# Last layer of a four-layer kernel: ScalarE copies the spread values out of PSUM, GpSimd makes the key-value products, the scans read them from SBUF

## The reference

```python
r = xr @ Wr; k = xk @ Wk; v = xv @ Wv
w_log = -jnp.exp(time_decay + jnp.tanh(xw @ decay_w1) @ decay_w2)
def fwd_step(S, inp):
    rt, kt, vt, wt = inp
    S = jnp.exp(wt)[..., None] * S + kt[..., None] * vt[..., None, :]
    return (S, jnp.einsum('bhk,bhkv->bhv', rt, S))
def bwd_step(S, inp):
    rt, kt, vt, wt = inp
    y = jnp.einsum('bhk,bhkv->bhv', rt, S)
    S = jnp.exp(wt)[..., None] * (S + kt[..., None] * vt[..., None, :])
    return (S, y)
y = y_f + y_b
y = y * jax.nn.sigmoid(dx @ gate_w + gate_b)   # then a norm over each head, times g, times Wo
```

## Time and profile before

| | us |
|---|---|
| median of 3 runs (lowest, highest) | 2316.47 (2316.39, 2316.59) |
| profiled execution, its own time | 2314.24 |
| its span, first to last instruction | 2312.5 |
| first forward scan of the last layer starts | 1997.20 |
| last backward scan starts | 2268.12 |
| mean granted TensorE clock, share of full speed | 0.945 |

### The profile page before, as it was taken

How to read it: one execution, slowest core, us unless ns; L and a number is a source line. 1 busy time by engine, 2 the same in 40 slices (tenths; PEclk the granted TensorE clock), 3 DMA queues, 4 the chain that set the end, 5 groups by cost and what they waited for, 6 DMA issues and landing times. The chain is left out here.

```text
span 2312.5 us, 56820 instructions
## 1 busy us (share of the span) xinstructions
PE 2062.4 (89%) x22888; PEld 1391.5 (60%) x22888; DVE 1623.5 (70%) x4129; ACT 1283.3 (55%) x2560; POOL 947.6 (41%) x1176
## 2 busy tenths in 40 slices
PE   4679998998999999999999796899999986889886
PEld 2448887996888887888887664344433333334233
DVE  7666664775666676667665563899898936698895
ACT  2247775565777777777776242267676763323323
POOL 2037776664678744665443032111111100154462
PEclk8789999999999999999999797699999997999998
DMA  6311113104011100000000063011111101000000
GB/s 180 106 64 38 39 38 97 50 29 149 21 39 19 35 3 20 2 21 3 3 2 2 16 205 106 16 43 49 38 37 38 40 4 38 0 0 9 0 9 19
DMA packets 77925, 94.14 MB, mean 41 GB/s; under 512 B 10145, under 2 KB 56242, under 8 KB 76002
## 3 DMA queue, kind: packets, MB, share of 16 engines
q1 hardware_dynamic: 64178, 77.23, 11.1%
q0 software_dynamic: 13488, 13.28, 2.9%
HBM read 54.55 MB, written 35.53 MB: 39 GB/s over the span
## 5 line engine op out<-in xcount | busy, mean ns | idle before, releaser
L1166 DVE TENSOR_REDUCE a_parts<-a_S 128x1 f32<-128x512 f32 (+1 forms) x576 | 363.0, 684 | 29.0 <-PE a_S L1050 22.7
L1137 ACT ACTIVATE WA<-a_E 128x1024 f32<-128x1024 f32 (+1 forms) x320 | 283.1, 940 | 117.9 <-PE a_E L1078 58.8
L1042 PE MATMUL a_S<-a_KS,a_QS 54*128 54x512 bf16 (+3 forms) x768 | 189.6, 348 | 31.0 <-DVE a_parts L1166 18.4
L463 POOL TENSOR_SCALAR WA<-WA,a1b_rinv 128x1024 f32<-128x1024 f32 (+3 forms) x192 | 142.5, 761 | 181.8 <-DVE a1b_rinv L802 181.6
L463 POOL TENSOR_SCALAR XR<-XR,a1b_rinv 128x768 f32<-128x768 f32 (+3 forms) x192 | 141.7, 752 | 118.9 <-DVE a1b_rinv L802 118.4
L618 PE MATMUL a1b_O<-a1b_PT,WA 128*64 128x128 f32 x3072 | 189.0, 276 | 0.0
L618 PEld LDWEIGHTS a1b_O<-a1b_PT,WA 128*64 128x64 f32 x3072 | 165.8, 137 | 6.5
L583 PE MATMUL a1b_B<-a1b_Kf,a1b_Qf 64*128 64x512 f32 (+2 forms) x768 | 156.2, 481 | 8.5 <-issue 4.6
L1042 PEld LDWEIGHTS a_S<-a_KS,a_QS 54*128 54x128 bf16 x768 | 58.7, 95 | 172.5 <-DVE a_parts L1166 136.0
L1090 PE MATMUL a_O<-WA,V 128*9 128x512 f32 (+3 forms) x1536 | 154.2, 489 | 0.1
L714 ACT ACTIVATE WA<-WA,a1b_nmax 128x1024 f32<-128x1024 f32 (+3 forms) x192 | 150.4, 792 | 1.3 <-DVE a1b_nmax L784 1.3
(11 more groups left out here) (533 smaller groups left out, 5890.9 us busy)
## 6 DMA issues: line engine op xcount, KB each, us to landing
WA<-in_w SPq DMA_DIRECT2D x8, 1024.0 KB, 9.0
a_QS<-qstack SPq DMA_DIRECT2D x32, 216.0 KB
a_KS<-kstack SPq DMA_DIRECT2D x32, 216.0 KB
a1b_tb<-tab SPq DMA_DIRECT2D x12, 512.0 KB
qstack<-f_parts SPq DMA_DIRECT2D x24, 256.0 KB
kstack<-f_parts SPq DMA_DIRECT2D x24, 256.0 KB
f_slots<-f1r_zrows SPq DMA_DIRECT2D x9, 516.0 KB
f1t_xs<-f_slots SPq DMA_DIRECT2D x9, 516.0 KB, 7.3
```

Of the source, the lines that this page charges most:

```text
L463: pool.tensor_scalar(v, v, rinv[:, e, u, part:part + 1], 1.0, ALU.mult, ALU.mult).then_inc(n_sb, 1)
L1042: ins = pe.matmul(pS[(at + half) % SB][:, lo:lo + n], QS[s][ROW[half], pair, i * P:(i + 1) * P], KS[s][ROW[half], pair, block * P:block * ...
L1137: act.activation(PT[q % NP][:, :, 0:w], pE[q % 2][:, :, 0:w], ACT.Exp).then_inc(e_sb, 1)
L1166: dve.tensor_reduce(peak, pS[at % SB][:, :].rearrange("p (c k) -> p c k", c=n), AX.X, ALU.max)\
```

## The change

Per step, the product of spread values and keys leaves VectorE. ScalarE copies the spread values from PSUM into an SBUF tile (`spread`, two of them, the memory of mdx and mxr), and GpSimd multiplies them with k into an SBUF tile `kv` (two of them), from which both scans read. TensorE's `values(n)` waits for the copy of step n - 2 where it waited for the scans of step n - 2. GpSimd makes the product of step n + 1 ahead of the sum of step n (`weigh`). The sum is written into Sr and multiplied there in place, so that Ss is gone. ScalarE's program of a batch is cut into eight parts with one copy behind each.

```diff
-    pV = kv = [ph.ps(f"V{i}", (P, T)) for i in range(2)]
+    pV = [ph.ps(f"V{i}", (P, T)) for i in range(2)]
+    NK, NV = 2, 2
+    kv = tile("kv", True)
+    flat = [m[:, :, :].rearrange("p s t -> p (s t)")[:, 0:T] for m in (mdx, mxr, mxk)]
+    spread = flat[0:2]
...
+            def weigh(n):
+                if n >= NS:
+                    return
+                b, v = divmod(n, HK)
+                if v == 0:
+                    pool.wait_ge(emptied["k"], 2 * b + 2)
+                pool.wait_ge(spread_sb, n + 1)
+                if n >= NK:
+                    pool.wait_ge(scanned, n - NK + 1)
+                elif n == 0:
+                    pool.wait_ge(l_delta, EARLY - 1)
+                pool.tensor_tensor(kv[n % NK][:, :], spread[n % NV][:, :], k[b % 2][:, :], ALU.mult).then_inc(kv_sb, 1)
+
+            weigh(0)
+            weigh(1)
             for b in range(B):
                 for v in range(HK):
                     n, s = b * HK + v, v % 2
+                    if n:
+                        weigh(n + 1)
                     if v == 0:
                         pool.wait_ge(emptied["r"], 2 * b + 2)
                     if n >= 2:
                         pool.wait_ge(y_ps, n - 1)
                     pool.wait_ge(scanned, n + 1)
-                    if n:
-                        pool.wait_ge(sr_sb, n)
-                    pool.tensor_tensor(Ss[:, :], Sf[s][:, :], Sb[:, s, 1:T + 1], ALU.add).then_inc(sum_sb, 1)
+                    pool.tensor_tensor(Sr[s][:, :], Sf[s][:, :], Sb[:, s, 1:T + 1], ALU.add).then_inc(sum_sb, 1)
                     pool.wait_ge(sum_sb, n + 1)
-                    pool.tensor_tensor(Sr[s][:, :], Ss[:, :], r[b % 2][:, :], ALU.mult).then_inc(sr_sb, 1)
+                    pool.tensor_tensor(Sr[s][:, :], Sr[s][:, :], r[b % 2][:, :], ALU.mult).then_inc(sr_sb, 1)
...
                 if n >= 2:
-                    pe.wait_ge(scanned, n - 1)
+                    pe.wait_ge(spread_sb, n - 1)
...
+            def spread_values(n):
+                if n >= NS:
+                    return
+                act.wait_ge(v_ps, n + 1)
+                if n >= NV:
+                    act.wait_ge(kv_sb, n - NV + 1)
+                else:
+                    act.wait_ge((l_mixed, l_rk)[n], EARLY)
+                act.copy(spread[n % NV][:, :], pV[n % 2][:, :]).then_inc(spread_sb, 1)
...
+                for v in range(HK):
+                    n = b * HK + v
+                    if v == 0:
+                        if b + 1 < B:
+                            begin(b + 1)
+                        if b:
+                            evacuate("cen", b - 1)
+                        if b + 1 < B:
+                            for kind in ("t5a", "t5b", "gate"):
+                                evacuate(kind, b + 1)
+                    if v == 1 and b:
+                        evacuate("var", b - 1)
+                        deviation(b - 1)
+                    if v == 2 and b + 1 < B:
+                        evacuate("d1", b + 1)
...
+                    if 4 <= v <= 6 and b + 1 < B:
+                        evacuate("krg"[v - 4], b + 1)
+                    if b + 1 < B or v + 2 < HK:
+                        spread_values(n + 2)
...
-                    dve.wait_ge(v_ps, n + 1)
                     if v == 0:
-                        dve.wait_ge(emptied["k"], 2 * b + 2)
                         dve.wait_ge(dec_sb, b + 1)
-                    dve.tensor_tensor(kv[s][:, :], pV[s][:, :], k[b % 2][:, :], ALU.mult).then_inc(kv_ps, 1)
                     if n >= 2:
                         dve.wait_ge(sum_sb, n - 1)
-                    dve.wait_ge(kv_ps, n + 1)
-                    dve.tensor_tensor_scan(Sf[s][:, :], dec[b % 2][:, :], kv[s][:, :], 0.0, ALU.mult, ALU.add)
-                    dve.tensor_tensor_scan(Sb[:, s, T - 1::-1], kv[s][:, ::-1], dec[b % 2][:, ::-1], 0.0,
+                    dve.wait_ge(kv_sb, n + 1)
+                    dve.tensor_tensor_scan(Sf[s][:, :], dec[b % 2][:, :], kv[n % NK][:, :], 0.0, ALU.mult, ALU.add)
+                    dve.tensor_tensor_scan(Sb[:, s, T - 1::-1], kv[n % NK][:, ::-1], dec[b % 2][:, ::-1], 0.0,
                                            ALU.add, ALU.mult).then_inc(scanned, 1)
```

More of the change, by code:

```diff
@@ L2112, in wkv @@
     Sf, Sr = (tile(n, True) for n in ("Sf", "Sr"))
-    Ss = tile("Ss")
     Sb = ph.sb("Sb", [P, 2, T + 1])
@@ L2124, in wkv @@
     mdx, mxr, mxk = (ph.sb(n, [P, 3, CH]) for n in ("mdx", "mxr", "mxk"))
+    flat = [m[:, :, :].rearrange("p s t -> p (s t)")[:, 0:T] for m in (mdx, mxr, mxk)]
     mkr = [Sf[0][:, 0:CH], Sf[0][:, CH:T], Sf[1][:, 0:CH]]
     mdelta = [Sr[0][:, 0:CH], Sr[0][:, CH:T], Sr[1][:, 0:CH]]
-    msig = [Sf[1][:, CH:T], Sr[1][:, CH:T], Ss[:, 0:CH]]
+    msig = [Sf[1][:, CH:T], Sr[1][:, CH:T], kv[0][:, 0:CH]]
+    spread = flat[0:2]
     low = [t[:, 0:CH] for t in (*pV, pY)]
@@ L2131, in wkv @@
         ph.sem(n) for n in ("ldx", "lmixed", "lrk", "lrelu", "lk2", "lsig", "lv", "ldelta", "ltr", "lx"))
-    stored = ph.sem("stored")
+    stored, spread_sb = ph.sem("stored"), ph.sem("spreadsb")
     rows_out = out.rearrange("(n p) d -> p n d", p=P)
@@ L2136, in wkv @@
     dx1, dx2, xv1, ln_sb, de_sb, yc_sb = (ph.sem(n) for n in ("dx1", "dx2", "xv1", "lnsb", "desb", "ycsb"))
-    v_ps, kv_ps, scanned, sum_sb, sr_sb, y_ps, c_ps = (
-        ph.sem(n) for n in ("vps", "kvps", "scanned", "sumsb", "srsb", "yps", "cps"))
+    v_ps, kv_sb, scanned, sum_sb, sr_sb, y_ps, c_ps = (
+        ph.sem(n) for n in ("vps", "kvsb", "scanned", "sumsb", "srsb", "yps", "cps"))
     KINDS = ("t5a", "t5b", "gate", "m_w", "m_k", "d1", "m_v", "d2", "m_r", "k", "m_g", "r", "g", "cen", "var", "out")
@@ L2434, in _ @@
             evacuate("g", 0)
+            spread_values(0)
+            spread_values(1)
             for b in range(B):
[L2436 to L2454, removed]
+                for v in range(HK):
[13 more added lines that the diff above has]
+                        evacuate("d1", b + 1)
+                    if v == 3:
+                        if b:
+                            shape(b - 1)
+                        if b + 1 < B:
+                            evacuate("d2", b + 1)
+                            decay(b + 1)
+                    if 4 <= v <= 6 and b + 1 < B:
+                        evacuate("krg"[v - 4], b + 1)
+                    if b + 1 < B or v + 2 < HK:
+                        spread_values(n + 2)
             evacuate("cen", B - 1)
@@ L2587, in _ @@
             gated(B - 1)
+            dve.wait_ge(kv_sb, NS)
             interpolate(4)
```

## The result

| | before | changed |
|---|---|---|
| median, us | 2316.43 (4 runs) | 2413.05 (4 runs, 2412.36 to 2413.82) |
| ratio, 95% interval | | 1.0425, [1.0411, 1.0438] |
| profiled execution's span, us | 2312.5 | 2411.3 |

The account below looks back on a forecast made before the run. VectorE was taken to bound the loop, except for a chain through all engines at batch starts. 25.7 + 2 x 23.1 + 38.5 = 110.4 us on 2314.24, plus 2.2 for the median, gave 2427 us; range 2385 to 2465.

Parts of the forecast that it names:

- The step that decides: Scans in the last layer's loop, now with two SBUF inputs, and SBUF-reading GpSimd instructions exclude each other by whole instructions.
- The cost of one step: Scan loop: five instructions of VectorE and GpSimd take turns at one port, 10.8 us a step (10.4 to 11.4).
- Steps 2 to 7 of batch 1: Six steps of 10.8 us plus normalisation and xv additions on the port: 68.0 us against 49.4, +18.6.
- The first two steps of a batch: Batch start, from scan v = 0 to scan v = 2: 31.6 us against 27.1, +4.5 (bounds +3 to +9).
- The walk: Batch start followed instruction by instruction from the end of product kv of v = 0; scan v = 2 starts at 31 to 33.
- Batch 3: Last batch, no next one to prepare: 50.0 us become 8 x 10.8 + 2.1 = 88.5, +38.5, the largest term.
- the first scan: Start of the loop: later by ScalarE's copy and GpSimd's product less VectorE's product, 2.3 us.
- batch 0: First batch of the loop: 92.7 us against 69.3, with steps 2 to 7 +20.4 and its start +3.
- the likeliest case: Scans and GpSimd exclude each other by whole instructions in the loop: 2427 us, bounds 2413 to 2455, chance 0.76.
- TensorE as a bound: Rival: TensorE at the lower clock presses on the steps, 5 to 25 us more a batch, 2455 us named, chance 0.08.
- The first rival: Scans don't take the port: about -6 us in each of three batches, 2306 us, faster by 0.5%, chance 0.11.
- Signs to look for: Expected profile: scans over 4 us, GpSimd maxima of 4, 10.5 to 11 between forward scans, VectorE busier, TensorE awaiting GpSimd.

Follow-up runs that it names:

- The run nearest to it: Changed kernel with both scans reading the spread values in PSUM instead of GpSimd's product in SBUF, TensorE waiting for the scans, product unused: 2326.86 us, ratio 1.0053.

## Why the prediction was right, and where it was not

- **The step that decides** held. The choice to carry the exclusion, seen only for additions and similar operations, over to scans was right: two runs that move the scans' operand between PSUM and SBUF, and no instruction from one engine to another, show it from both sides (+39 us into SBUF, -86 us out of it).
- **The cost of one step** was 10.8 us and measured 10.52 where five instructions follow strictly. The terms came to 10.66, and 0.14 was added for an order that didn't come. The scans took 2.15 and 2.16 us where 2.09 and 2.07 were counted, the multiplications 2.13 where 2.21 were, the sum 1.95 for 2.00, and the 0.08 between two instructions of one engine was not paid.
- **Steps 2 to 7 of batch 1**: 64.8 for 68.0. Six steps of 10.52 and the 3.2 us of other two-input work would be 66.3. But only the last two of the six have that length: from forward scan to forward scan they took 10.9, 15.4, 7.8, 9.6, 10.5 and 10.5 us. The rest is attributed, untested, to stretches in which VectorE works out of PSUM while GpSimd runs ahead.
- **The first two steps of a batch**: 34.2 for 31.6, inside the bounds of +3 to +9. The walk held up to the scans of v = 1: `begin` ended 18.8 us after the product (18.6 forecast), both scans 23.2 after it (23.1). The predicted stall of GpSimd was there too: it waited 14.4 us for the copy behind the evacuation of `gate`, and that copy waited last for TensorE's values. But the mix of w ended at 34.4, not near 31.5: VectorE waited 9.6 us for m_w's matmul, which began 12.6 us after the last matmuls of `t5a` began; before it was 9.9. Of these 2.8 us the walk lacked two things. TensorE waited 1.4 us for ScalarE's evacuation of `var`, which now stands behind the new copy; and matmuls ran longer at the lower level (3.62 us for 2.70 in one group; the granted clock of the two steps was 0.73, and 0.94 before). Before:

```profile
2079.72 1.95 PE L2222 MATMUL a_C<-a_x,WA 128*128 128x512 f32 x2 [1.14 <-DVE a_x L2476]
2081.60 2.70 PE L2224 MATMUL a_C<-a_x,WA 128*32 128x512 f32 x4
```

and after, TensorE and ScalarE:

```profile
2107.09 2.04 PE L2241 MATMUL a_C<-a_x,WA 128*128 128x512 f32 x2 [1.14 <-DVE a_x L2513]
2109.06 3.62 PE L2243 MATMUL a_C<-a_x,WA 128*32 128x512 f32 x4
...
2119.73 1.98 PE L2252 MATMUL a_C<-a_t5a,WA 128*128 128x512 f32 x4 [1.39 <-ACT a_rs L2412]
...
2116.66 1.01 ACT L2447 COPY a_mdx<-a_V 128x1024 f32<-128x1024 f32 x1 [0.78 <-PE a_V L2284]
2117.70 1.28 ACT L2412 ACT_TABLE_LOAD   x1
2118.99 1.27 ACT L2412 ACTIVATE a_rs<-a_C,a_geps 128x512 f32<-128x512 f32 x2
```

- **Batch 3** was 83.9 for 88.5, the largest error of a term. Seven steps, too long by 0.28 us each, make 2.0 of it. The other 2.5 is a slip of the count: the last step was taken whole, at 10.8 us, but from its forward scan's start to its backward scan's end it lasts 8.3.
- **How near the sum came is in part luck.** The parts missed by 1.1 us at the first scan, 2.8 in batch 0, 0.7 in batch 1, 1.6 in batch 2, 4.6 in batch 3 and 0.9 behind the loop, all on the high side. In batch 1 a start taken too short and later steps taken too long nearly cancelled, in batch 2 by half. The remaining 2.2 us were added for the distance of the median from the profiled execution, which the changed kernel's runs don't show. The result lies at the low end of the likeliest case's own bounds (2413 to 2455).
- **TensorE as a bound** did not come in the later six steps of a batch: in those of batch 1 VectorE waited for GpSimd's product only. TensorE's busy time grew from 67 to 77 us a batch of 99, since more of it ran at the lower level. At a batch's start it is part of the chain, as shown above.
- **The first rival, free scans at 2306 us, was mis-sized**, though its mechanism is the one a port of its own would give. The run nearest to it measured 2326.86, on the other side of before. Its -6 us in each of three batches rested on the sentence that the loop is bound by VectorE, read from shares of whole batches. In the six steps concerned TensorE had 2.2 us free, not 9; 6.8 of the 9 us are at the batch's start. With the scans in PSUM again VectorE was busy 42.3 us in these steps where it had been 46.5, TensorE 49.0 of 49.9, and nothing was gained. The forecast itself didn't hang on it, as the port made a longer bound than either.
- **Signs to look for**: scans over 4 us, GpSimd's two multiplications over 4, VectorE's busy time up, ScalarE's copies at 1.01 us without VectorE ever waiting on them, all seen. Three came otherwise. GpSimd's sum was expected to reach 4 us as well; its median stayed at 1.99 and its longest was 2.98, because it mostly follows GpSimd's own product. The 10.5 to 11 us between forward scans from v = 2 on held in three of the six steps of batch 1. And TensorE's matmuls into Y waited for GpSimd 16 times in 32 steps, not in nearly every one.

## What to carry to other kernels

Before moving an operand or an instruction, count for each step the VectorE instructions with two SBUF inputs and the GpSimd instructions that read SBUF, and add their times as if they ran on one engine: here 4.3 + 6.2 = 10.5 us a step, while each engine alone had room. A scan operand left in PSUM was worth 86 us of 2413, more than the 39 us of VectorE time that the edit removed. And read the bound from the stretch in question: shares over a batch hid that TensorE had no room in six of its eight steps.

## What the runs showed of the hardware that was not expected

- A 128x1024 multiplication on GpSimd takes 2.35 us and an addition 2.00, undisturbed: so for r, for kv (2.347) and for the normalisation (2.353), whatever tiles they read.
- An instruction that waits for the port loses little: it ends 2.13 to 2.16 us after the other's end, against 2.26 to 2.35 from a free start, as if its start-up were hidden in the wait.
- A GpSimd fill that only writes 128x1024 took 943 to 954 ns beside scans that waited for GpSimd's other instructions in the same step, and such a scan ended as soon with the fill beside it (2.15 us after the multiplication) as without (2.14).
